# TensorE filler matmuls at the layer borders of a four-layer decoder kernel

## The chip, the cores and the metric

The kernel runs on one NeuronCore of one Trainium2 chip. The metric is the device time of one execution in microseconds, as the median of several runs. A core has a tensor engine (TensorE, PE in the profile; its weight loads are PEld), a vector engine (VectorE, DVE), a scalar engine (ScalarE, ACT), GpSimd (POOL) and a sync engine (SyncE, SP) that issues DMAs. Each engine runs its own list of instructions in order, and engines wait for each other on semaphores.

## The reference, cut to what matters

The input x is 8 sequences of 128 tokens with 128 features in f32. Twelve layers each add to x a function of its layer norm:

```python
x = x + _L0_attn_ref(_layernorm(x, axis=-1), ...)            # L0a: gated, ternary weights
x = x + _L0_xattn_ref(_layernorm(x, axis=-1), ctx, ctx, ...)  # L0x: attention over ctx, rotary
x = x + _L0_ffn_ref(_layernorm(x, axis=-1), ...)              # L0f: 8 experts, top 2
x = x + _L1_attn_ref(_layernorm(x, axis=-1), ...)             # L1a: causal attention
x = x + _L1_xattn_ref(_layernorm(x, axis=-1), ctx, ...)       # L1x: attention with a distance bias
x = x + _L1_ffn_ref(_layernorm(x, axis=-1), ...)              # L1f: 6 experts, top 2, GELU
x = x + _L2_attn_ref(_layernorm(x, axis=-1), ...)             # L2a: linear attention and an inner MLP
x = x + _L2_xattn_ref(_layernorm(x, axis=-1), ctx, ctx, mask, ...)  # L2x: masked attention
x = x + _L2_ffn_ref(_layernorm(x, axis=-1), ...)              # L2f: 16 experts, top 8, SwiGLU
x = x + _L3_attn_ref(_layernorm(x, axis=-1), ...)             # L3a: causal attention, rotary
x = x + _L3_xattn_ref(ctx, ctx, _layernorm(x, axis=-1), ...)  # L3x: one-head attention
x = x + _L3_ffn_ref(_layernorm(x, axis=-1), ...)              # L3f: light and heavy MLP, 50-step router
return x
```

## The kernel before

Everything stays in SBUF. The 8 sequences are split into two groups of 4 (g is 0 or 1), and each group has its own tiles (x, xn, xnT, QT, KT, big and so on) and its own four of the eight PSUM banks (banks_of(g), 512 f32 columns each; bank(i) is the group's i-th). For every engine a generator program(g) lists one group's instructions, layer after layer, and yields a key (layer number, phase) before each piece. weave() merges the two generators in the order of these keys, so each engine's order is written by hand. A step that others wait for is marked with s.step(name), and s.at(name, group) gives the semaphore and the count for pe.wait_ge. Functions ahead() and BEHIND put the entry of group 0 into L0f, L1x, L1f, L2x, L2f and L3x ahead of the end of group 1's previous layer.

Each layer border has the same chain: VectorE adds the layer's output to x (L1289, L1335 or L1347), takes means and variances (L1165 to L1170, mark "var"), GpSimd raises the variance to -0.5 (L332, mark "var_r"), VectorE writes xn (L1360, mark "xn"), TensorE transposes it in four pieces (turn_rows, L415), ScalarE copies it to xnT (L866), and TensorE projects it (mm, L399). The attention layers (attend) loop over 8 half-units per group and end with back() (L468), the normalisation on VectorE (L1245 to L1255, marks "co2" and "co3"), and out_proj (the transposes of co, ScalarE's copy coT, and the projection "y").

The borders that have more in them are L0x (rotary with square roots, marks "qv", "qraw", "qrot", "krot"), L2a (marks "co3", "coT"), L2f (gate_up(c) waits for VectorE's product of the chunk before, "mul"), L3x (a softmax, marks "sub", "exp", "p") and L3f (router: marks "ms", "rs", "xr").

The mask of an attention layer is already applied as the filler is built: a bf16 identity (identb, 128 by 128) times a bf16 constant of 128 by 512 columns, into one bank (masked, L440). An f32 matmul of the source appears in the profile as two MATMUL records, a transpose or a bf16 one as one.

Of the kernel before, what the change touches and what calls it, by code (L numbers as in the profile page):

```python
# [10 lines left out]
ALU = mybir.AluOpType  # L11
# [80 lines left out]
def build(nc, x_d, ctx_d, mask_d, w_d, r_d, c_d, k_d, b_d, out_d, marks):  # L92
# [112 lines left out]
    def four(t):  # L205
        return t.rearrange("p (b d) -> p b d", b=GB)
# [47 lines left out]
    def beat(turn, k=0):  # L254

        return 30 + 10 * turn + k
# [140 lines left out]
    def _(pe):  # L397
# [7 lines left out]
        def program(g):  # L405
# [12 lines left out]
            def project_rows(bk, srcT, weight, name):  # L418
# [2 lines left out]
                    ins = mm(seq(bk, b), srcT[:, b * P:(b + 1) * P], weight)  # L421
                ins.then_inc(*s.step(name))

            def project_cols(bk, srcT, weight, name):

                mm(bank(bk), weight, srcT[:, :]).then_inc(*s.step(name))
# [87 lines left out]

            def out_proj(n, l, weight):
                yield n, (beat(2 * GB - 1, 8) if g == 0 else 130)
                pe.wait_ge(*s.at(f"{l}.co{GB - 1}"))
                turn_rows(3 * g, t.co, "coTp")
                yield n, (beat(2 * GB + 1, 1) if g == 0 else 131)
                pe.wait_ge(*s.at(f"{l}.coT"))  # L520
                project_rows(3 - 3 * g, t.coT, weight, "y")

# [27 lines left out]
            for n, l in enumerate(LAYERS[1:STAGES + 1]):  # L550
# [20 lines left out]
                    ins.then_inc(*s.step("zwp"))  # L571
                if l not in ("L0a", "L3f"):
                    yield n, (BEHIND[l] if g and l in BEHIND else 2)
                    pe.wait_ge(*s.at(f"{l}.xn"))
                    turn_rows(3, xn, "xnTp")
                if l == "L0a":
                    yield n, 2
                    pe.wait_ge(loaded[f"ctx{g}"], 16)
                    turn_rows(3, t.cin, "cTp")
                    yield n, 4  # L580
                    pe.wait_ge(*s.at("L0a.q3"))
                    pe.wait_ge(*s.at("L0a.q3a"))
                    for j in range(3):
                        for b in range(GB):
                            ins = pe.transpose(seq(j, b), t.ta[:, j * GB + b, :], ident)  # L585
                    ins.then_inc(*s.step("q3Tp"))
                    if g == 0:
                        pe.wait_ge(*s.at("L0a.ctxT", 1))
                        pe.wait_ge(*p.at("pre.ones"))
                        pe.wait_ge(*p.at("pre.wabs"))  # L590
                        mm(ps[:, 7 * 512:7 * 512 + 4], ones[:, :], wabs[:, :]).then_inc(*p.step("wsum"))
                    yield n, 6
                    pe.wait_ge(*p.at("pre.wtern"))
                    pe.wait_ge(*s.at("L0a.q3T"))
                    for j in range(3):
                        for b in range(GB):
                            ins = mm(seq(j, b), t.qT3[:, j, b * P:(b + 1) * P], wtern[:, j * P:(j + 1) * P])
                    ins.then_inc(*s.step("ifg"))
                    if g == GROUPS - 1:
                        yield n, 7  # L600
                        pe.wait_ge(*p.at("pre.gwn"))
                        pe.transpose(bank(3)[:, 0:E2], gwn[:, :], ident[0:E2, 0:E2]).then_inc(*p.step("gwTp"))
                    yield n, 12.5
                    pe.wait_ge(*s.at("L0a.ctxT"))
                    if g == 0:
                        pe.wait_ge(loaded["L0x"], 16)
                    pe.wait_ge(*s.at("L0a.ms1"))
                    project_rows(2, ctxT, w("L0x_wk"), "k")
                    yield n, 14
                    if g == GROUPS - 1:  # L610
                        pe.wait_ge(*p.at("pre.gwT"))
                    pe.wait_ge(*s.at("L0a.qo"))
                    pe.wait_ge(*s.at("L0a.qoa"))
                    turn_rows(3, t.ta, "qoTp")
                    yield n, 16
                    pe.wait_ge(*s.at("L0a.qoT"))
                    for b in range(GB):
                        ins = mm(seq(1, b), t.qT3[:, 0, b * P:(b + 1) * P], wtern[:, 3 * P:4 * P])
                    ins.then_inc(*s.step("y"))
                if l in ("L0x", "L3a"):  # L620
                    yield n, 4
                    pe.wait_ge(*s.at(f"{l}.xnT"))
                    project_rows(0, xnT, w(f"{l}_wq"), "q")
                    if l == "L3a":
                        project_rows(1, xnT, w("L3a_wk"), "k")
                        project_rows(2, xnT, w("L3a_wv"), "v")
                    if l == "L0x" and g == 0:
                        yield n, 6
                        turn_keys()
                    yield n, 8  # L630
                    pe.wait_ge(*s.at(f"{l}.qrot"))
                    turn_rows(0, t.tc, "QTp")
                    if l == "L3a":
                        pe.wait_ge(*s.at("L3a.krot"))
                        turn_rows(1, t.td, "KTp")
                    elif g == GROUPS - 1:
                        turn_keys()
                    yield n, 20
                    yield from attend(n, l)
                    yield from out_proj(n, l, w(f"{l}_wo"))  # L640
# [56 lines left out]
                if l == "L2a":  # L697
# [28 lines left out]
                    for h in range(MH):  # L726
# [2 lines left out]
                            ins = mm(bank(h)[:, b * (MD + 1):(b + 1) * (MD + 1)], pr[:, GB * h + b, :], t.vv[:, b, h, :])  # L729
                        ins.then_inc(*s.step(f"O{h}"))  # L730
                    yield n, (22, 24.5)[g]
                    pe.wait_ge(*s.at("L2a.co3"))
                    turn_rows(2, t.co, "coTp")
                    yield n, (22.7, 26)[g]
                    pe.wait_ge(*s.at("L2a.coT"))
                    project_rows(3, t.coT, w("L2a_wo"), "y")
                    yield n, (25, 30)[g]
# [12 lines left out]
                if l == "L2f":  # L750
# [11 lines left out]

                    for c in range(LEAD):
                        yield n, 5 + 4 * c
                        gate_up(c)
                    yield n, 16
                    pe.wait_ge(*s.at("L2f.gws"))
# [23 lines left out]
                if l == "L3x":  # L791
# [7 lines left out]
                        ins = mm(seq(3, b), QT[:, b * P:(b + 1) * P], KT[:, b * P:(b + 1) * P])  # L799
                    ins.then_inc(*s.step("S"))  # L800
                    yield n, 10
                    pe.wait_ge(*s.at("L3x.p"))
                    turn_rows(0, pr, "Tp")
                    yield n, 12
# [6 lines left out]
                    pe.wait_ge(*s.at("L3x.coT"))  # L811
                    project_rows(2, t.coT, w("L3x_wo"), "y")
                if l == "L3f":
                    if g == GROUPS - 1:
                        yield n, 3
                        pe.wait_ge(*s.at("L3f.rs", 0))
                        pe.wait_ge(*s.at("L3f.rs"))
                        pe.transpose(bank(2)[0:B, 0:P], rt_s[:, :], ident).then_inc(*s.step("sT"))
# [288 lines left out]
    def _(dve):  # L1107
# [50 lines left out]
        def program(g):  # L1158
# [169 lines left out]
            def mix(n, l, experts, banks, phase):  # L1328

                for e in experts:  # L1330
# [6 lines left out]
                    if e == experts[len(experts) // 2 - 1]:  # L1337
# [3 lines left out]
                        dve.tensor_tensor(x[:, :, :], four(bank(3)), x[:, :, :], ALU.add).then_inc(*s.step())  # L1341
                        dve.wait_ge(*s.last())
                dve.wait_ge(*s.last())
                if l == "L0f":
                    yield n, 199
                    dve.wait_ge(*s.at(f"L0f.sum{E0 - 2}"))
                    dve.tensor_tensor(x[:, :, :], four(t.hid[:, 0, :]), x[:, :, :], ALU.add).then_inc(*s.step())  # L1347
                    dve.wait_ge(*s.last())

            for n, l in enumerate(LAYERS[1:STAGES + 1]):  # L1350
# [438 lines left out]
```

## Time and profile before

| | |
|---|---|
| time, 3 runs | 690.33 us median (690.32 to 691.32) |
| span of the profiled execution | 688.3 us |
| mean granted TensorE clock | 0.902 |
| PE busy | 548.8 us (80%), 4258 instructions |
| PEld busy | 375.4 us (55%) |
| DVE busy | 468.2 us (68%) |
| ACT busy | 259.3 us (38%) |
| POOL busy | 98.3 us (14%) |
| chain that ended last | PE 64%, DVE 19%, ACT 10%, POOL 2%, issue 2%, DMA 1% |

The span is from the first to the last instruction of one execution. A granted clock of 1.0 is 2.4 GHz and one of 0.5 is 1.2 GHz. In a row of the timeline the first number is the start in us, the second the time of the merged group in us, then come engine, line, operation, output and inputs, shapes and count; in brackets stands how long the engine was idle before and what released it.

### The profile page before, as it was taken

To read this page: it belongs to the slowest core of one execution; us is meant where nothing else is said; L and a number is where in the kernel's file an instruction comes from. 1 tells how busy PE (TensorE), PEld (TensorE's weight loads), DVE (VectorE), ACT (ScalarE), POOL (GpSimd) and SP (SyncE) were. 2 spreads that over 40 slices of the span, in tenths; PEclk is the share of its full clock that TensorE was granted. 3 is DMA by queue.
4 is the path that set the end of the run, shared out by engine and by line. 5 is a ranking of instruction groups with operands and counts; after the bars stand their busy time and mean duration, and the time that the engine had idled before them with its cause. 6 is when DMAs were issued, how large, how long until landed. Compare 5 with 4: busy or idle time off the path is not lost.

```text
span 688.3 us, 10667 instructions
## 1 busy us (share of the span) xinstructions
PE 548.8 (80%) x4258; PEld 375.4 (55%) x4265; DVE 468.2 (68%) x1200; ACT 259.3 (38%) x422; POOL 98.3 (14%) x101
## 2 busy tenths in 40 slices
PE   1436489787689899968996889997799968998487
PEld 0325255686355656655775765556345654565335
DVE  7688688757588777765246745886644378866685
ACT  2365544315244434435332423453321124442270
POOL 5021220004310051000002014200100012002120
PEclk9756699969899999998997999999899989998779
DMA  8900000000000000000000000000000000000001
GB/s 281 371 0 2 0 1 2 1 1 1 0 1 2 1 1 1 2 1 1 0 2 1 0 1 1 1 2 1 0 1 0 1 0 2 1 2 0 0 0 31
DMA packets 6720, 12.40 MB, mean 18 GB/s; under 512 B 528, under 2 KB 4880, under 8 KB 6288
## 3 DMA queue, kind: packets, MB, share of 16 engines
q1 hardware_dynamic: 6672, 11.73, 4.7%
q8 instruction: 33, 0.54, 0.3%
q14 instruction: 15, 0.12, 0.1%
HBM read 11.21 MB, written 0.52 MB: 17 GB/s over the span
## 4 chain that ended last, share of the span: by engine, by line
PE 64%; DVE 19%; ACT 10%; issue 2%; POOL 2%; DMA 1%; SPq 1%; DVEq 0%; ACTq 0%
PE ps L399 47%; PE ps L452 11%; ACT big L897 5%; PE ps L415 4%; DVE st L1165 2%; PE ps L468 2%; DVE big L1276 1%; DVE mx L1272 1%; POOL rs L332 1%; DVE xn L1360 1%; DMA co<-in_ctx 1%; DVE x L1289 1%; PE ps L585 1%; DVE mv L1168 1%; ACT xnT L866 1%
## 5 line engine op out<-in xcount | busy, mean ns | idle before, releaser
L897 ACT ACTIVATE big<-ps 128x1024 f32<-128x1024 f32 x80 | 81.8, 1024 | 109.0 <-PE ps L452 109.0
L1272 DVE TENSOR_REDUCE mx<-ps 128x8 f32<-128x1024 f32 x80 | 97.5, 1219 | 27.9 <-PE ps L399 27.9
L1276 DVE TENSOR_TENSOR big<-ps,mx 128x1024 f32<-128x1024 f32 x80 | 98.0, 1225 | 6.9
L452 PEld LDWEIGHTS ps<-kt,big 128*128 128x128 f32 x640 | 71.0, 141 | 39.0 <-DVE big L1276 28.2
L452 PE MATMUL ps<-kt,big 128*128 128x128 f32 x640 | 85.2, 276 | 5.6 <-DVE big L1276 5.6
L332 POOL TENSOR_TENSOR rs<-ve,negh 128x4 f32<-128x4 f32 x26 | 26.4, 1015 | 393.1 <-DVE ve L1170 393.0
L399 PE MATMUL ps<-xnT,wt 128*128 128x512 f32 (+1 forms) x140 | 73.2, 654 | 5.9 <-DVE big L1552 2.8
L399 PEld LDWEIGHTS ps<-wt,big 128*128 128x128 f32 (+1 forms) x480 | 56.0, 191 | 8.5 <-issue 7.9
L399 PE MATMUL ps<-wt,big 128*128 128x128 f32 (+1 forms) x480 | 60.3, 279 | 0.0
L399 PE MATMUL ps<-big,vaug 128*32 128x128 f32 x1280 | 51.5, 279 | 10.9 <-ACT big L897 10.9
L351 POOL TENSOR_TENSOR KTm<-qk,kt 128x512 f32<-128x512 f32 x34 | 37.4, 1107 | 105.2 <-PE ps L399 62.3
L399 PE MATMUL ps<-bt 128*128 128x512 bf16 (+1 forms) x185 | 48.5, 352 | 1.3 <-issue 0.9
L399 PE MATMUL ps<-KTm,qk 32*128 32x512 f32 x320 | 46.6, 652 | 0.0
L866 ACT ACTIVATE xnT<-ps 128x512 f32<-128x512 f32 (+1 forms) x40 | 19.6, 489 | 71.1 <-PE ps L415 66.2
L399 PEld LDWEIGHTS ps<-big,vaug 128*32 128x32 f32 x1280 | 30.1, 109 | 29.0 <-ACT big L897 22.5
L399 PEld LDWEIGHTS ps<-xnT,wt 128*128 128x128 f32 (+1 forms) x140 | 26.0, 204 | 32.8 <-issue 21.3
L1335 DVE SCALAR_TENSOR_TENSOR x<-ps,gw,x 128x128 f32<-128x128 f32 x80 | 22.3, 344 | 29.8 <-PE ps L399 29.1
L399 PE MATMUL ps<-wt,xnT 128*128 128x128 f32 (+2 forms) x256 | 38.3, 312 | 4.1 <-ACT xnT L866 2.7
L1289 DVE TENSOR_TENSOR x<-ps,x 128x512 f32<-128x512 f32 x16 | 11.1, 692 | 44.4 <-PE ps L399 44.4
L399 PEld LDWEIGHTS ps<-wt,xnT 128*128 128x128 f32 x256 | 36.9, 229 | 7.2 <-ACT xnT L866 4.2
L1360 DVE TENSOR_SCALAR xn<-x,mv,rs 128x128 f32<-128x128 f32 x96 | 28.1, 357 | 9.0 <-POOL rs L332 8.3
L415 PE MATMUL ps<-kt,xn 128*128 128x128 f32 x80 | 17.1, 353 | 19.7 <-DVE xn L1360 19.6
(275 smaller groups left out, 772.1 us busy)
## 6 DMA issues: line engine op xcount, KB each, us to landing
wt<-in_weights SPq DMA_DIRECT2D x1, 1664.0 KB, 17.2
wt<-in_weights SPq DMA_DIRECT2D x1, 1603.0 KB, 12.0
wt<-in_weights SPq DMA_DIRECT2D x6, 256.0 KB, 11.1
bt<-in_bconsts SPq DMA_DIRECT2D x1, 1024.0 KB, 8.5
rowt<-in_rows SPq DMA_DIRECT2D x1, 975.0 KB, 6.7
wt<-in_weights SPq DMA_DIRECT2D x1, 832.0 KB, 13.5
wt<-in_weights SPq DMA_DIRECT2D x1, 608.0 KB, 18.4
wt<-in_weights SPq DMA_DIRECT2D x1, 580.0 KB, 5.6
```

Of the source, the lines that this page charges most:

```text
L332: pool.tensor_tensor(out, src, negh[:, :], ALU.pow).then_inc(*s.step(name + "_r"))
L351: pool.tensor_tensor(t.KTm[:, b % 2, :, :], keys_of(t, b), own_head(), ALU.mult).then_inc(*s.step(f"keys{b}"))
L399: return pe.matmul(out, lhsT, rhs, start=start, stop=stop, **k)
L415: ins = pe.transpose(seq(bk, b), src[:, b, :], ident)
L452: ins = pe.transpose(heads_of(pair(g, u % 2))[:, j // HG, j % HG, :], pr[:, (u % 2) * HH + j, :], ident)
L866: act.activation(out, src, ACT.Copy).then_inc(*s.step(name))
L897: act.activation(PT[:, half * HH:(half + 1) * HH, :].rearrange("p (i j) k -> p i j k", i=2), heads_of(pair(g, half)), ACT.Exp, scale=SCALE ...
L1272: dve.tensor_reduce(top, S, AX.X, ALU.max).then_inc(*s.step())
L1276: dve.tensor_tensor(pr[:, half * HH:(half + 1) * HH, :].rearrange("p (i j) k -> p i j k", i=2), S, top.unsqueeze(3).to_broadcast([P, 2, HG ...
L1289: dve.tensor_tensor(x[:, :, :], four(bank(bk)), x[:, :, :], ALU.add).then_inc(*s.step(name))
L1335: dve.scalar_tensor_tensor(x[:, b, :], bank(banks[e])[:, b * P:(b + 1) * P], gw[:, b, e:e + 1], x[:, b, :], ALU.mult, ALU.add).then_inc(*s ...
L1360: dve.tensor_scalar(xn[:, b, :], x[:, b, :], t.mv[:, b, 0:1], t.rs[:, b:b + 1], ALU.subtract, ALU.mult).then_inc(*s.step("xn"))
```

## The change

A helper filler(k, out) issues k matmuls of identb and identb repeated four times (bf16, 128 by 512 columns) into a bank whose content nobody needs at that point; filler_behind(name, ...) first waits for a named step of another engine, then issues them. No output of a filler is read. There are 176 of them: 13 at the entry of L0x, L1a, L2a and L3a for group 0 (5 behind the previous layer's x, 4 behind var, 4 behind var_r), 10 or 5 at the end of each of the five attention layers for group 1 (8 or 3 before the wait for co3, 2 before the wait for coT), 2 behind the transposes of xn in L0f, L1f, L2f and L3x for each group, 21 in L0x, 8 inside L2a, 7 in L2f, 8 in L3x and 24 in L3f for group 0. Two marks are added on VectorE (L0f.x and L1f.x) so that they can be waited for. Apart from these and the waits of filler_behind no instruction is added, removed or moved.

```diff
--- before.py
+++ after.py
@@ -420,6 +420,15 @@
                 for b in range(GB):
                     ins = mm(seq(bk, b), srcT[:, b * P:(b + 1) * P], weight)
                 ins.then_inc(*s.step(name))
+
+            def filler(k, out):
+
+                for _ in range(k):
+                    mm(out, identb, identb.unsqueeze(1).to_broadcast([P, HG, P]))
+
+            def filler_behind(name, k, out, group=None):
+                pe.wait_ge(*s.at(name, group))
+                filler(k, out)
 
             def project_cols(bk, srcT, weight, name):
 
@@ -514,9 +523,13 @@
 
             def out_proj(n, l, weight):
                 yield n, (beat(2 * GB - 1, 8) if g == 0 else 130)
+                if g == GROUPS - 1:
+                    filler(8 if LAYERS[n + 2] in ("L0f", "L1f", "L2f") else 3, banks_of(0)(0))
                 pe.wait_ge(*s.at(f"{l}.co{GB - 1}"))
                 turn_rows(3 * g, t.co, "coTp")
                 yield n, (beat(2 * GB + 1, 1) if g == 0 else 131)
+                if g == GROUPS - 1:
+                    filler(2, banks_of(0)(0))
                 pe.wait_ge(*s.at(f"{l}.coT"))
                 project_rows(3 - 3 * g, t.coT, weight, "y")
 
@@ -571,8 +584,14 @@
                     ins.then_inc(*s.step("zwp"))
                 if l not in ("L0a", "L3f"):
                     yield n, (BEHIND[l] if g and l in BEHIND else 2)
+                    if g == 0 and l in ("L0x", "L1a", "L2a", "L3a"):
+                        filler_behind(f"{LAYERS[n]}.x", 5, bank(3))
+                        filler_behind(f"{l}.var", 4, bank(3))
+                        filler_behind(f"{l}.var_r", 4, bank(3))
                     pe.wait_ge(*s.at(f"{l}.xn"))
                     turn_rows(3, xn, "xnTp")
+                    if l in ("L0f", "L1f", "L2f", "L3x"):
+                        filler(2, bank(0))
                 if l == "L0a":
                     yield n, 2
                     pe.wait_ge(loaded[f"ctx{g}"], 16)
@@ -628,12 +647,19 @@
                         yield n, 6
                         turn_keys()
                     yield n, 8
+                    if l == "L0x":
+                        if g == 0:
+                            filler_behind("L0x.qv", 5, bank(3))
+                            filler_behind("L0x.qraw", 5, bank(3))
+                        else:
+                            filler(5, bank(3))
                     pe.wait_ge(*s.at(f"{l}.qrot"))
                     turn_rows(0, t.tc, "QTp")
                     if l == "L3a":
                         pe.wait_ge(*s.at("L3a.krot"))
                         turn_rows(1, t.td, "KTp")
                     elif g == GROUPS - 1:
+                        filler(6, bank(3))
                         turn_keys()
                     yield n, 20
                     yield from attend(n, l)
@@ -729,9 +755,12 @@
                             ins = mm(bank(h)[:, b * (MD + 1):(b + 1) * (MD + 1)], pr[:, GB * h + b, :], t.vv[:, b, h, :])
                         ins.then_inc(*s.step(f"O{h}"))
                     yield n, (22, 24.5)[g]
+                    if g:
+                        filler(4, bank(3))
                     pe.wait_ge(*s.at("L2a.co3"))
                     turn_rows(2, t.co, "coTp")
                     yield n, (22.7, 26)[g]
+                    filler(2, bank(3))
                     pe.wait_ge(*s.at("L2a.coT"))
                     project_rows(3, t.coT, w("L2a_wo"), "y")
                     yield n, (25, 30)[g]
@@ -762,6 +791,8 @@
 
                     for c in range(LEAD):
                         yield n, 5 + 4 * c
+                        if c == 2 and g == 0:
+                            filler(7, bank(2))
                         gate_up(c)
                     yield n, 16
                     pe.wait_ge(*s.at("L2f.gws"))
@@ -799,6 +830,9 @@
                         ins = mm(seq(3, b), QT[:, b * P:(b + 1) * P], KT[:, b * P:(b + 1) * P])
                     ins.then_inc(*s.step("S"))
                     yield n, 10
+                    if g == 0:
+                        filler_behind("L3x.sub", 4, bank(0))
+                        filler_behind("L3x.exp", 4, bank(0))
                     pe.wait_ge(*s.at("L3x.p"))
                     turn_rows(0, pr, "Tp")
                     yield n, 12
@@ -811,6 +845,13 @@
                     pe.wait_ge(*s.at("L3x.coT"))
                     project_rows(2, t.coT, w("L3x_wo"), "y")
                 if l == "L3f":
+                    if g == 0:
+                        yield n, 2
+                        filler_behind("L3x.x", 4, bank(3))
+                        filler_behind("L3f.var", 5, bank(3))
+                        filler_behind("L3f.var_r", 5, bank(3))
+                        filler_behind("L3f.xn", 5, bank(3))
+                        filler_behind("L3f.ms", 5, bank(3))
                     if g == GROUPS - 1:
                         yield n, 3
                         pe.wait_ge(*s.at("L3f.rs", 0))
@@ -1341,10 +1382,12 @@
                         dve.tensor_tensor(x[:, :, :], four(bank(3)), x[:, :, :], ALU.add).then_inc(*s.step())
                         dve.wait_ge(*s.last())
                 dve.wait_ge(*s.last())
+                if l == "L1f":
+                    marks[g, "L1f.x"] = marks[g, f"L1f.x{E1 - 1}.{GB - 1}"]
                 if l == "L0f":
                     yield n, 199
                     dve.wait_ge(*s.at(f"L0f.sum{E0 - 2}"))
-                    dve.tensor_tensor(x[:, :, :], four(t.hid[:, 0, :]), x[:, :, :], ALU.add).then_inc(*s.step())
+                    dve.tensor_tensor(x[:, :, :], four(t.hid[:, 0, :]), x[:, :, :], ALU.add).then_inc(*s.step("x"))
                     dve.wait_ge(*s.last())
 
             for n, l in enumerate(LAYERS[1:STAGES + 1]):
```

## Rows read from the trace of the kernel before

**Rows 1.** The page, its second part: 40 equal slices of the span, tenths busy or granted.

```profile
PE   1436489787689899968996889997799968998487
PEclk9756699969899999998997999999899989998779
```

**Rows 2.** Stretches with low granted clock: us, busy (x count) by engine, PEclk, DMA.

```profile
61.97:85.86 23.89, 12.83 (x54) 8.23 (x55) 17.31 (x39) 11.33 (x17) 4.83 (x5) 0.64 0.00 0
137.06:150.72 13.66, 11.93 (x52) 10.88 (x52) 7.46 (x36) 1.19 (x2) 1.01 (x1) 0.50 0.00 1
174.60:181.43 6.83, 3.83 (x11) 2.43 (x12) 3.83 (x23) 1.19 (x2) 2.05 (x2) 0.50 0.00 1
307.73:314.55 6.82, 6.13 (x19) 4.00 (x18) 5.01 (x27) 0.82 (x2) 1.01 (x1) 0.50 0.00 0
365.75:376.00 10.25, 7.08 (x20) 5.67 (x21) 5.43 (x19) 2.48 (x3) 4.20 (x4) 0.50 0.01 2
399.88:403.30 3.42, 2.87 (x13) 2.87 (x14) 0.51 (x3) 1.37 (x2) 0.00 (x0) 0.50 0.00 0
488.63:492.04 3.41, 3.41 (x5) 0.90 (x5) 0.95 (x3) 2.63 (x4) 0.00 (x0) 0.50 0.00 0
498.87:502.29 3.42, 3.42 (x5) 1.35 (x4) 2.36 (x12) 0.60 (x1) 0.00 (x0) 0.50 0.00 0
553.49:560.31 6.82, 4.77 (x21) 4.40 (x22) 3.67 (x17) 1.19 (x2) 1.68 (x2) 0.50 0.00 0
625.16:632.00 6.84, 6.15 (x18) 3.69 (x17) 3.89 (x14) 1.88 (x3) 3.15 (x3) 0.50 0.00 0
638.82:645.64 6.82, 5.11 (x23) 4.72 (x24) 2.66 (x11) 1.79 (x3) 0.00 (x0) 0.50 0.00 0
652.47:662.71 10.24, 6.02 (x13) 2.64 (x14) 8.28 (x53) 6.89 (x15) 4.22 (x4) 0.50 0.00 0
```

**Rows 3.** Timeline, four bf16 matmuls of 512 columns each, at either clock.

```profile
81.31 1.91 PE L399 MATMUL ps<-bt 128*128 128x512 bf16 x4
568.53 1.03 PE L399 MATMUL ps<-bt 128*128 128x512 bf16 x4
```

**Rows 4.** Timeline, PE, group 1 transposes of co in L0x and in L2x.

```profile
137.42 1.11 PE L415 MATMUL ps<-kt,co 128*128 128x128 f32 x4 [2.74 <-DVE co L1255]
479.20 0.66 PE L415 MATMUL ps<-kt,co 128*128 128x128 f32 x4 [2.74 <-DVE co L1255]
```

**Rows 5.** Timeline, PE, entry of L0x: transposes of xn, projection of q.

```profile
63.63 0.66 PE L415 MATMUL ps<-kt,xn 128*128 128x128 f32 x4 [1.86 <-DVE xn L1360]
65.37 3.58 PE L399 MATMUL ps<-wt,xnT 128*128 128x128 f32 x16
```

**Rows 6.** Timeline, L0f: gates and experts of group 0, of group 1; gates read.

```profile
142.83 7.19 PE L399 MATMUL ps<-wt,xnT 128*128 128x8 f32 x32 [0.69 <-ACT xnT L866]
151.55 3.84 PE L399 MATMUL ps<-wt,xnT 128*128 128x8 f32 x32 [0.69 <-ACT xnT L866]
152.71 0.19 DVE L1297 TENSOR_TENSOR lg<-ps,rowt 128x32 f32<-128x32 f32 x1 [3.88 <-PE ps L399]
```

**Rows 7.** Timeline, PE, L1f: first expert of group 0.

```profile
311.44 3.50 PE L399 MATMUL ps<-xnT,wt 128*128 128x512 f32 x4
```

**Rows 8.** Timeline, PE, L2a: feature projections of both groups.

```profile
370.95 9.57 PE L399 MATMUL ps<-zw,xnT 128*128 128x256 f32 x32
```

**Rows 9.** Timeline, PE, L2f: third gate and up chunks, both groups.

```profile
498.42 5.40 PE L399 MATMUL ps<-xnT,wt 128*128 128x512 f32 x8 [2.80 <-DVE big L1552]
```

**Rows 10.** Timeline, PE, L3a: projections of q, k and v, both groups.

```profile
557.54 6.85 PE L399 MATMUL ps<-wt,xnT 128*128 128x128 f32 x48
```

**Rows 11.** Timeline, PE, L3x: weighted values of both groups.

```profile
642.55 3.43 PE L399 MATMUL ps<-big,tc 128*128 128x128 f32 x16
```

**Rows 12.** L3f: piece of the chain (start, us, what); timeline, last router step.

```profile
659.10 11.05 PE ps L399 x20
677.87 0.28 DVE L1650 TENSOR_TENSOR rt_e<-rt_b,rt_r 8x128 f32<-8x128 f32 x1
```

## The prediction

> **What bounds the kernel now.** I read the page's slices first: PE's digits are 8 and 9 in the attention loops and 4 to 7 at the borders between layers, and PEclk drops just there [rows 1]. Then I asked for the granted clock by stretches and cut them where it changes. Behind the first layer there are twelve stretches with a low clock, 102.4 us in all, and in eleven of them it stands at 0.50, which is 1.2 GHz [rows 2]. In every one TensorE had been idle for some us while VectorE, GpSimd and ScalarE did the layer norm, a softmax or a gate. Outside them the clock is 1.0, so attention loops and expert loops have nothing to gain. What a low clock costs is seen best where both groups do the same work: gates and three experts take 7.19 us for group 0 and 3.84 us for group 1 [rows 6], four masks 1.91 against 1.03 us, four transposes 1.11 against 0.66 us [rows 3, 4]. So the question at each border is which part of PE's slow work the next layer waits for, and whether the fillers keep the clock up without being late themselves.
>
> **What the fillers cost.** Four matmuls of the filler's shape take 1.03 us at the high and 1.91 us at the low clock [rows 3]; their starts are some 0.22 and 0.43 us apart, as the last one's way through the array is in these times too. 176 fillers are then 39 us of PE at the high clock, against 688.3 - 548.8 = 139.5 us in which PE is idle. They are placed ahead of waits, and where the wait behind them is longer than they are, they cost nothing. Two behind the transposes of xn take 0.43 us while ScalarE's copy and its hand-over leave PE 0.69 us idle [rows 6]: nothing. The eight ahead of co3 take 1.7 us in an idle time of 2.74 us [rows 4]: nothing. Seven in L2f take 1.5 of 2.80 us [rows 9]: nothing. Cover is too short at two places. At the entry of L0x 13 fillers (2.8 us) stand in an idle time of 1.86 us, and x is ready before PE arrives [rows 5]: +0.95 us. In L2a two fillers stand directly ahead of group 1's y, whose coT is already there: +0.4 us. The added waits are on steps that the old wait for xn, qrot, p or xr includes, so nothing queued behind them on PE is held longer than before. VectorE, ScalarE, GpSimd and the DMA queues get no new instruction or wait; two named marks on VectorE are free. Were the clock low, a filler would be 0.43 us and these covers fail: that is the rival below.
>
> **What a held clock gives, border by border.** The bound of each is half the PE time of its stretch [rows 2]: 73.6/2, less what is already fast in the first one, about 35 us. The path takes less of it:
> - L0x: q's projections 3.58 to 1.8 us [rows 5], less the 0.95; before the first scores the transposed keys (0.45), four masks (0.9) and as much again in scores (0.9) [rows 3, 4]. -3.1.
> - L0x to L0f: the transposes of co (0.45), y (8 records; 16 such take 3.43 us at the low clock [rows 11], so 0.85 less), transposes of xn (0.45), gates and experts 7.19 to 3.84 (3.35), group 1's transposes (0.45) [rows 4, 6]. -5.5. VectorE idled 3.88 us for group 1's gates [rows 6], so it follows.
> - L0f to L1a: transposes and the first projections, of 3.83 us busy [rows 2]; -1.4.
> - L1x to L1f: the first expert's 3.50 us [rows 7] fall by 1.75, gates and transposes by 0.6; -2.35 of at most 3.07.
> - L1f to L2a: VectorE waits for the first quarter of the 9.57 us of feature projections [rows 8], all of which is slow; with the transposes -2.2. Behind that VectorE is busy without a break, so more of PE's 3.5 us isn't worth anything.
> - inside L2a: 1.1 of at most 1.4, less the 0.4 of the two fillers; -0.65.
> - L2f: in 488.63 to 492.04 PE is wholly busy, but the next chunk waits for VectorE's product; I take 0.25 of 1.7. In 498.87 to 502.29 all 8 records of [rows 9] are on the path: -1.7. Together -1.95.
> - L2f to L3a: transposes and q of group 0 (a sixth of the 48 records [rows 10]), then VectorE's rotations bind; -1.45 of 2.4.
> - L3a to L3x: 6.15 us busy, but group 1's xn comes at its own time; -1.5 of 3.1.
> - L3x: transposes and 3.43 us of weighted values [rows 11]; -1.8 of 2.55.
> - L3f: from 659.10 PE has no gap for 11.05 us [rows 12] and is slow to 662.71: -2.6 of 3.0. What is late next is the router, whose last step ends at 678.15 [rows 12]. PE asks for it only in the second half of group 1's y, at the very end of the layer, so I take PE's asking to stay behind it; nearly all of the room is used up.
> Sum: -24.5 us, with bounds of -35 (all slow PE time on the path) and 0.
>
> **Does the clock hold?** The trace has no filler in an idle border. What it shows is that the same idle time can go either way: after 2.74 us group 1's transposes of co run slow in L0x (1.11 us) and fast in L2x (0.66 us) [rows 4]. So fillers that cut such a stretch into pieces should mostly hold it, and some borders will still fall. I take as lost: L0f to L1a, where x comes late and PE is idle before the first filler (no 1.4, and eight fillers at 0.43 us between var and xn, about 1.1 late); half of L3f (1.3), since PE idles again behind its last transposes; and 2.0 for one more border of mean size. That leaves 24.5 - 5.8 = 18.7 us.
>
> The Trainium skill bears on this twice, and no term above needs it. "TensorE: Matmul & The Clock Gate", section Terms, prices a throttled time at that time times one minus its share of the clock; with the lengths and clocks of [rows 2] that would be about 48 us and 642 us, an estimate by that page. The rows speak for half of it, as PE is idle in 29 us of those stretches and VectorE sets part of the rest. The same page, "Part 4: PE-mode transpose", states that transposes don't count as activity for the gate in the way that matmuls do; this speaks for borders that fall in spite of some work in them, and for matmuls as fillers. No row here separates the two.
>
> **Rivals.**
> 1. The clock holds at few borders (the idle pieces between x, var, var_r and xn are still too long, or fillers put off a fall instead of preventing it). The L0x to L0f border, the one with the most fillers in one block, and two or three small ones remain: -5.5, -2.5, against +1 of late fillers: 690.3 - 7 = 683.3. For it: the two fates of one idle time [rows 4]. Against it: the fillers fill half or more of most idle pieces.
> 2. The clock holds everywhere, and PE's earlier work lets the engines behind it start earlier too: -24.5 to -28, about 664. Against it: VectorE's own chain, which sets L2a, L3a and L3x.
> 3. Slower: the fillers don't lift the clock at all, and run at 0.43 us each in front of real work. L0x: 13 take 5.6 us against 1.86 idle, +3.7. L1a, L2a, L3a: the eight behind var and var_r take 3.4 us where some 2.3 us are free, +1.1 each. The pairs behind xn's transposes, 0.86 against 0.69 us [rows 6], eight times +0.17. L2a +0.8. Sum about +9: 699. It decides from the point where lateness (9) exceeds what the borders that do hold give back; a third of the 24.5 us is enough to cancel it. Against it: 4 masks of the same form stand in the attention loops, where the clock is high all along.
> 4. The change doesn't do what it says, for instance because a filler's wait is met too late to matter: then 690, a chance of 3 in 100.
>
> **How the numbers follow.** The profiled execution spans 688.3 us and the median is 690.33, so 2.0 us lie around the span and stay. Forecast: 690.3 - 18.7 = 671.6 us, chance 0.67, by itself 666 to 678 (one or two borders more or fewer). Rival 1: 0.15, rival 2: 0.09, rival 3: 0.06, rival 4: 0.03. The range reaches to both neighbours and leaves out half of each: 663.5 to 683.5. Within 0.2% (1.4 us, about what a measurement of this kernel can tell from no change) is rival 4 alone. Faster 0.91, same 0.03, slower 0.06.
>
> **What would show it.** Twelve low stretches become four or five, and the mean granted clock rises from 0.902 to 0.95 or more. Gates and experts of group 0 in L0f take 3.9 us as those of group 1 do; VectorE's wait before group 1's gates goes. Fillers start 0.22 us apart. PE busy rises by 39 us and falls by what runs faster. At the entry of L0x the transposes of xn follow the fillers without a gap. The prediction is wrong if low stretches still stand at most borders, or if they are gone and the borders are as long as before because VectorE or ScalarE set them.

## The result

The changed kernel takes 670.0 us (median of 4 runs, 667.1 to 671.91) against 690.33 us (4 runs, 688.23 to 691.32): a ratio of 0.972, 95% interval 0.969 to 0.976. The forecast was 671.6 us. The profiled execution was the longest of the four (671.91 us), its span 670.1 against 688.3 us; so the trace explains 18.2 of the 20.3 us. Two executions further on were in a slower state of the chip, one of the kernel without fillers (845.6 us) and one of the kernel before (699.8 us), and the ratios below leave them out (the medians include them, which moves these by less than 0.5 us).

The page of the changed kernel; first the engine's busy time and then the 40 slices, to be held against [rows 1]:

```profile
span 670.1 us, 11020 instructions
PE 561.8 (84%) x4434; PEld 370.8 (55%) x4441; DVE 467.6 (70%) x1200; ACT 260.0 (39%) x422; POOL 98.5 (15%) x101
...
PE   1426689878999999988998889998799978998787
...
PEclk9967999998999999999999999999999999999989
```

PEclk is 9 nearly everywhere; the mean granted clock is 0.971 instead of 0.902. There are 176 more PE instructions, as many as fillers, and PE is busy only 13 us longer, as the fillers' time is mostly made up for by the real work that runs faster. Behind L0a four low stretches are left against the twelve of [rows 2], where the forecast had four or five; the last 2 us of each span are low too and left out. The first row of the next fence is for comparison, the others are these four (columns as in [rows 2]):

```profile
62.00:149.51 87.51, 74.03 (x701) 48.21 (x699) 72.02 (x150) 35.77 (x56) 10.42 (x10) 1.00 0.00 1
149.51:156.34 6.83, 6.28 (x30) 6.10 (x29) 3.94 (x15) 5.17 (x20) 2.50 (x2) 0.50 0.01 2
166.58:169.99 3.41, 3.18 (x8) 1.09 (x9) 3.27 (x21) 0.00 (x0) 1.02 (x1) 0.50 0.01 2
552.28:555.70 3.42, 3.42 (x13) 0.82 (x10) 0.77 (x2) 1.88 (x2) 1.54 (x1) 0.50 0.00 0
641.03:644.44 3.41, 3.37 (x4) 1.13 (x5) 3.08 (x19) 3.00 (x4) 0.00 (x0) 0.50 0.00 0
```

Two of them are new: in the trace of the kernel before the clock was high at the experts of L0f (149.51 here) and at the first masks and scores of L3a (552.28 here).

The L0x to L0f border, timeline of PE and the first read of group 1's gates on VectorE:

```profile
130.66 1.89 PE L399 MATMUL ps<-bt 128*128 128x512 bf16 x8
133.57 0.66 PE L415 MATMUL ps<-kt,co 128*128 128x128 f32 x4 [1.02 <-DVE co L1296]
134.06 0.59 PE L399 MATMUL ps<-bt 128*128 128x512 bf16 x2
134.91 1.16 PE L399 MATMUL ps<-wt,coT 128*128 128x128 f32 x8 [0.26 <-ACT coT L907]
135.91 0.60 PE L415 MATMUL ps<-kt,xn 128*128 128x128 f32 x4
136.34 0.59 PE L399 MATMUL ps<-bt 128*128 128x512 bf16 x2
137.19 3.84 PE L399 MATMUL ps<-wt,xnT 128*128 128x8 f32 x32 [0.26 <-ACT xnT L907]
...
142.15 3.84 PE L399 MATMUL ps<-wt,xnT 128*128 128x8 f32 x32 [0.26 <-ACT xnT L907]
...
143.63 0.19 DVE L1338 TENSOR_TENSOR lg<-ps,rowt 128x32 f32<-128x32 f32 x1
```

The bf16 rows are the fillers. The idle time ahead of the transposes of co is 1.02 us instead of 2.74 [rows 4], that ahead of gates and experts 0.26 instead of 0.69 us, and the real work behind them is not late. Gates and experts of group 0 take 3.84 instead of 7.19 us [rows 6]. VectorE reads group 1's gates 9.1 us earlier than before (143.63 against 152.71), and no longer waits for them.

To place the gain I took instructions that both traces have on VectorE and subtracted their starts. This difference is the lead of the changed kernel. The table has the lead over the kernel before, after each border, and its change (all in us):

| stretch | forecast term | lead after it | change |
|---|---|---|---|
| L0x | -3.1 | 3.86 | -3.86 |
| L0x to L0f | -5.5 | 9.08 | -5.22 |
| experts of L0f | none | 6.33 | +2.75 |
| L0f to L1a | taken as lost, +1.1 | 7.66 | -1.33 |
| L1x to L1f | -2.35 | 9.98 | -2.32 |
| L1f to L2a | -2.2 | 12.19 | -2.21 |
| inside L2a | -0.65 | 13.04 | -0.85 |
| L2f | -1.95 | 15.08 | -2.04 |
| L2f to L3a | -1.45 | 16.36 | -1.28 |
| first scores of L3a | none | 14.71 | +1.65 |
| L3a to L3x | -1.5 | 16.65 | -1.94 |
| L3x | -1.8 | 18.03 | -1.38 |
| L3f | -1.3 of 2.6 | 18.14 | -0.11 |

### The profile page after: what moved, and what is told of

Read it like the earlier page. It is cut to its first block, busy times and chain, and to the rows that moved or that the text cites. A ratio compares the mean times of both kernels' runs of the same rounds, so it can differ in the third digit from the quotient of the medians.

```text
span 670.1 us, 11020 instructions
## 1 busy us (share of the span) xinstructions
PE 561.8 (84%) x4434; PEld 370.8 (55%) x4441; DVE 467.6 (70%) x1200; ACT 260.0 (39%) x422; POOL 98.5 (15%) x101
## 4 chain that ended last, share of the span: by engine, by line
PE 59%; DVE 23%; ACT 11%; POOL 2%; issue 2%; DMA 1%; SPq 1%; DVEq 0%; ACTq 0%
PE ps L399 43%; PE ps L461 11%; ACT big L938 5%; DVE st L1206 3%; PE ps L415 3%; PE ps L477 2%; DVE xn L1403 2%; POOL rs L332 2%; DVE big L1317 1%; DVE mx L1313 1%; DVE x L1330 1%; DMA co<-in_ctx 1%; DVE mv L1209 1%; PE ps L604 1%; DVE ve L1211 1%
## 5 line engine op out<-in xcount | busy, mean ns | idle before, releaser
L399 PE MATMUL ps<-bt 128*128 128x512 bf16 (+1 forms) x361 | 94.0, 369 | 9.1 <-DVE ve L1211 3.1
L399 PE MATMUL ps<-xnT,wt 128*128 128x512 f32 (+1 forms) x140 | 66.5, 602 | 4.8 <-DVE big L1595 2.6
L399 PEld LDWEIGHTS ps<-bt 128*128 128x128 bf16 x368 | 32.3, 99 | 47.1 <-issue 18.5
L399 PEld LDWEIGHTS ps<-big,vaug 128*32 128x32 f32 x1280 | 30.1, 109 | 29.0 <-ACT big L938 22.5
L399 PEld LDWEIGHTS ps<-xnT,wt 128*128 128x128 f32 (+1 forms) x140 | 23.8, 187 | 28.3 <-issue 19.1
L399 PE MATMUL ps<-wt,xnT 128*128 128x128 f32 (+2 forms) x256 | 34.0, 291 | 3.1 <-DVE big L1551 1.5
L399 PEld LDWEIGHTS ps<-wt,xnT 128*128 128x128 f32 x256 | 32.7, 207 | 6.7 <-ACT xnT L907 3.0
```

Source lines behind the costliest of these rows:

```text
L399: return pe.matmul(out, lhsT, rhs, start=start, stop=stop, **k)
```

## The experiments

The theory: everything comes from TensorE's granted clock, and it takes wide matmuls in the idle times to hold it. The rivals: the gain comes from the added waits; any instruction on TensorE will do; the borders aren't separate; fillers cost more than the table shows. Each ratio is to runs of the kernel before on the same chip.

**Waits without fillers.** The fillers are left out, nothing else.

```diff
             def filler(k, out):
-                for _ in range(k):
-                    mm(out, identb, identb.unsqueeze(1).to_broadcast([P, HG, P]))
+                return
```

> The changed kernel with all 176 filler matmuls left out, its added waits kept. Theory (the gain is TensorE's clock alone): as the kernel before, 690 us, within 1 us, and the low-clock stretches of before return at the same borders. Rival A (part of the gain is that TensorE has already passed the earlier semaphores when xn comes, or sits on the waits differently): 3 us or more below 690.

Measured: 690.65 us, ratio 0.999 (0.996 to 1.003). The waits do nothing that can be told from noise, and the gain is the fillers'. Its profiled execution, with a span of 684.1 us, shows more. Stretch and timeline of PE at the L0x to L0f border:

```profile
139.92:153.34 13.42, 9.45 (x78) 8.22 (x76) 11.20 (x59) 2.27 (x7) 1.01 (x1) 1.00 0.00 1
```

```profile
137.12 0.66 PE L415 MATMUL ps<-kt,co 128*128 128x128 f32 x4 [2.74 <-DVE co L1295]
...
140.74 3.84 PE L399 MATMUL ps<-wt,xnT 128*128 128x8 f32 x32 [0.69 <-ACT xnT L906]
```

Without one filler, behind the same 2.74 us of idle time as in [rows 4], the clock stayed up here, where it had fallen in the profiled execution of the kernel before. So which borders fall differs between executions of the same work, and a border's term is what it costs when it falls, not what it costs every time. In the runs that the comparisons use, the kernel before took 685.6 to 694.7 us.

**Narrow fillers.** As many instructions, 8 columns each.

```diff
-                    mm(out, identb, identb.unsqueeze(1).to_broadcast([P, HG, P]))
+                    mm(out[:, 0:8], identb, identb[:, 0:8])
```

> All 176 fillers kept as instructions, each with 8 instead of 512 columns. The theory (clock, and for that the streamed columns of the fillers): 690 us, within 1.5 us, mean granted clock near 0.90. Rival B (any instruction on TensorE keeps the clock up, or an engine that isn't idle starts the real matmuls sooner): most of the 20 us gain remains, 670 to 675 us, clock 0.97.

Measured: 687.71 us, ratio 0.997 (0.994 to 1.001), mean clock 0.909 in the profiled execution. 176 more instructions with weight loads don't hold the clock; the same number with 512 columns does. As a narrow filler is also much shorter, this doesn't tell columns from busy time. The median lies 2.1 us under that of the kernel before (689.81 us here), where I had allowed 1.5; the interval includes no difference.

**Transposes as fillers.** Two f32 transposes of the identity in the place of each matmul.

```diff
-                for _ in range(k):
-                    mm(out, identb, identb.unsqueeze(1).to_broadcast([P, HG, P]))
+                for _ in range(2 * k):
+                    pe.transpose(out[:, 0:P], ident, ident)
```

> Each filler matmul is replaced by two f32 transposes of the identity, 128 columns each (four transposes took 0.66 us, so two are about 0.22 us apart as one filler is). If TensorE's clock takes transposes for work as it takes matmuls: 670 us, within 3 us, clock 0.97. If, as the Trainium skill (TensorE: Matmul & The Clock Gate, Part 4) states, transposes don't count in the same way: 688 us or more, for the fillers then run at 0.43 us a pair in front of real work, up to 699 us.

Measured: 670.98 us, ratio 0.970 (0.966 to 0.975), clock 0.971. The L0x to L0f border:

```profile
130.74 1.91 PE L427 MATMUL ps<-kt 128*128 128x128 f32 x16
133.64 0.66 PE L415 MATMUL ps<-kt,co 128*128 128x128 f32 x4 [1.00 <-DVE co L1296]
...
137.27 3.84 PE L399 MATMUL ps<-wt,xnT 128*128 128x8 f32 x32 [0.25 <-ACT xnT L907]
```

Sixteen transposes (line 427 of this kernel is the filler) take the time of eight fillers, and hold the clock as well: VectorE's leads agree with those of the changed kernel within 0.2 us to the end. Here the measurement decides against the page: the Trainium skill ("TensorE: Matmul & The Clock Gate", Part 4: PE-mode transpose) says that the full clock doesn't engage for transposes, as they don't count as activity in the same way. F32 transposes held it in this kernel, and they raised it too. In this trace the clock is low from 166.71 to 170.12 us, at the entry of L1a, and TensorE does nothing else in this time than these transposes, the first 15 of this row:

```profile
166.91 4.58 PE L427 MATMUL ps<-kt 128*128 128x128 f32 x26 [2.30 <-DVE x L1390]
```

Behind it the clock is 1.0, while the rest of them run.

**Twice as many.** Each group of fillers twice as long (range(2 * k)).

> Every filler group twice as long (352 matmuls). Theory: the clock is held at a few more borders (at most the 4 us still lost), but the fillers no longer fit into the idle times: at the entry of L0x 26 take 5.6 us (+2.8 more), pairs behind xn's transposes become 0.87 against 0.69 us (8 times +0.2), 16 ahead of co3 take 3.5 against 2.7 us (3 times +0.8), the 8 and 8 behind var and var_r fill 3.5 of 2.3 us (3 times +1.2), 14 in L2f 3.0 against 2.8. Sum about +12, so 675 to 684 us. Rival (lateness is hidden behind other engines): 670 or below.

Measured: 677.05 us, ratio 0.981 (0.976 to 0.985), clock 0.996. The clock is held as good as everywhere in the profiled execution, and the kernel is 5.5 to 7 us slower than with half of them. The entry of L0x:

```profile
61.58 6.16 PE L399 MATMUL ps<-bt 128*128 128x512 bf16 x26
67.57 1.04 PE L415 MATMUL ps<-kt,xn 128*128 128x128 f32 x8
```

The transposes of xn start at 67.57 instead of 63.99 us, and VectorE keeps these 3.5 us; 13 more fillers at 0.22 us are 2.8 of them, and the rest is the clock's, which rose at 62.3 instead of 60.8 us here. At the other borders doubling costs 0.1 to 1 us each, in L3f about 2, and where the clock is now held, or is low for a shorter time, 1.1 to 1.6 us come back (experts of L0f, L3a, L3f). 677 lies in the expected 675 to 684, at its low end: the sum of 12 us was too large.

**Half as many.** 95 matmuls, range((k + 1) // 2).

> Every filler group halved (8 to 4, 5 to 3, 4 to 2, 2 to 1 and so on, 95 matmuls in all). Theory (the clock needs enough work in each idle time): several borders fall again and half to two thirds of the gain is left, 676 to 682 us. Rival (any break in the idle time is enough): 670 us or, with less lateness, 669.

Measured: 680.78 us, ratio 0.986 (0.982 to 0.990), clock 0.924 in the profiled execution: half of the gain, as expected (676 to 682). The L1x to L1f border:

```profile
299.76 1.57 PE L399 MATMUL ps<-wt,coT 128*128 128x128 f32 x8 [0.47 <-ACT coT L907]
...
304.60 3.76 PE L399 MATMUL ps<-xnT,wt 128*128 128x512 f32 x4
```

One filler ahead of coT and four ahead of co3 don't hold it: y is slow in part, the first expert wholly (3.76 us, as the 3.50 of [rows 7]). With 95, 176 and 352 fillers the times are 681, 670 to 671.5 and 677: too few lose the clock, too many are late.

**One border alone.** Only the 14 fillers of the L0x to L0f border. Against the changed kernel:

```diff
-                if g == GROUPS - 1:
+                if g == GROUPS - 1 and l == "L0x":
                     filler(8 if LAYERS[n + 2] in ("L0f", "L1f", "L2f") else 3, banks_of(0)(0))
...
-                    if l in ("L0f", "L1f", "L2f", "L3x"):
+                    if l in ("L0f",):
                         filler(2, bank(0))
```

(and the other groups left out)

> Only the 14 fillers of the L0x to L0f border kept (8 ahead of co3 and 2 ahead of coT for group 1, 2 behind the transposes of xn for each group). Theory by my sum: 5.2 to 5.5 us faster than the kernel before in a trace where this border is slow before, so 684.5. Theory of luck (a border that is held only moves the fall to another one): 1 to 3 us faster. No gain at all would say that the borders aren't separate terms.

Measured: 685.39 us against 690.4 us, ratio 0.995 (0.991 to 0.998): 5 us by the medians, as the term says; but the interval reaches from 1 to 6 and so takes in the 1 to 3 us of the theory of luck. In the trace VectorE gains 5.3 us on the kernel before at this border, gives back 0.9 in the experts of L0f, where the clock falls from 152.88 to 156.29 us, and ends 4.7 us ahead. So the border is worth about its term, and a part of it is lost again right behind it. One such trace doesn't show that the fillers did it: the kernel without any gained 5.2 us at this border in its profiled execution and gave back 1.2. No other border was tested alone; that their terms add up is read from the table and not shown by an experiment.

**L3f.** This border gave 0.11 us of the 1.3. In the changed kernel (PE, then VectorE's wait for the transposed router weights):

```profile
639.64 0.66 PE L415 MATMUL ps<-kt,tc 128*128 128x128 f32 x4 [0.51 <-ACT tc L1125]
641.07 10.94 PE L399 MATMUL ps<-qk,wt 128*64 128x512 f32 x20 [0.78 <-ACT qk L1133]
...
664.19 0.17 DVE L1696 COPY rt_f<-ps 128x8 f32<-128x8 f32 x1 [4.08 <-PE ps L885]
```

The transposes behind the fillers are fast, then PE idles again and the clock falls at 641.03, just ahead of the long block, which takes 10.94 us as it took 11.05 before [rows 12]. The block starts 18.03 us earlier than before, which is the lead on entering L3f, so the fast transposes ahead of it brought nothing by themselves. Either the clock is missing here, or the router binds. Three kernels on one chip:

> The changed kernel once more, beside the next three on the same chip, for comparison: 670 us.

> The 24 fillers of L3f left out, with their waits. In the changed kernel's trace L3f is as long as before (VectorE's lead of 18.03 us on entering it is 18.14 us at the end). Theory X (they hold the clock only up to the router's transposes and lose it before the long block of projections): the same as the changed kernel, 670 us, within 1 us. Theory Y (they hold it in most executions and the profiled one was unlucky): 1.5 to 2.5 us slower.

> Nine more fillers in L3f: 4 behind ms, and 2 and 3 behind the transposes of the normalised rows of each group, where TensorE was idle 1.02, 0.51 and 0.78 us. If the clock is what L3f lacks: the block of 8 slow projections falls from 3.4 to 1.7 us and the kernel by 1.5 to 2.6 us, to 668. If the 50-step router binds as soon as the projections are earlier: less than 0.5 us.

```diff
-                        filler_behind("L3f.ms", 5, bank(3))
+                        filler_behind("L3f.ms", 9, bank(3))
...
                     turn_rows(3, t.tc, "xrTp")
+                    filler(2 + g, bank(0))
```

Measured: the changed kernel 671.51 us (ratio 0.973), without L3f's fillers 670.51 us (0.972), with nine more 669.04 us (0.970). The intervals, each some 0.004 to either side, overlap; so the medians alone don't tell the three apart, and the traces have to. With nine more:

```profile
638.85 0.81 PE L399 MATMUL ps<-bt 128*128 128x512 bf16 x3
639.79 9.31 PE L399 MATMUL ps<-qk,wt 128*64 128x512 f32 x20
```

```profile
661.28 0.17 DVE L1697 COPY rt_f<-ps 128x8 f32<-128x8 f32 x1 [2.44 <-PE ps L886]
```

The block falls to 9.31 us, and the kernel's end follows by the same 1.64 us (its lead over the changed kernel goes from 1.26 us in the router's steps to 2.91 us at the last product). VectorE still waits 2.44 us for PE, so the router doesn't bind. The 24 fillers of L3f as they stand are worth nothing that shows: they fill the time up to ms and leave the last two gaps open.

**More fillers where the clock still falls.**

```diff
+                if l == "L0f":
+                    filler_behind("L0f.lgs", (7, 2)[g], bank(3))
                 pe.wait_ge(*s.at(f"{l}.gw"))
...
+                    if g == 0 and l == "L1a":
+                        filler_behind("L0f.x5.3", 7, bank(3))
...
+                    if l == "L3a" and g:
+                        filler(5, bank(3))
                     pe.wait_ge(*s.at(f"{l}.qrot"))
                     turn_rows(0, t.tc, "QTp")
                     if l == "L3a":
+                        if g:
+                            filler(6, bank(3))
```

(and the nine of L3f; 36 in all, where the expectation counts 38)

> The changed kernel with 38 more fillers where its traces still show a low clock: 7 and 2 ahead of the transposed gates in L0f (group 0, group 1), 7 ahead of L1a behind VectorE's step x5.3, 5 and 6 in L3a's rotation for group 1, and the 9 of L3f. Theory: L0f gives back the 2.8 us it lost in the profiled execution, L3a up to 1.65, L3f 1.5 to 2.5; together 4 to 6 us less than the changed kernel, 665 us. Rival (a late filler costs what the clock gives): 669 to 671.

Measured: 667.58 us, ratio 0.968 (0.964 to 0.971), on another chip than the run above. That is 3.9 us less than the 671.51 and 2.4 less than the 670.0 of the changed kernel, under the 4 to 6 that were expected. In its trace VectorE gains 2.75 us on the changed kernel in L0f, 1.64 us at the first scores of L3a and 1.64 us in L3f, and gives back 1.42 us in L3x, where the clock now falls.

```diff
                     yield n, 4
+                    if g:
+                        filler(9, bank(0))
+                        filler_behind("pre.wtern", 16, bank(0))
+                        filler_behind("L0a.q3_s", 6, bank(0))
                     pe.wait_ge(*s.at("L0a.q3"))
...
+                    if g == 0:
+                        filler(8, bank(0))
+                        filler_behind("L0a.qo_s", 4, bank(0))
+                    else:
+                        filler(5, bank(0))
                     pe.wait_ge(*s.at("L0a.qo"))
```

> The same with 48 more fillers in L0a, where the clock is low from 24 to 61 us in every trace: 31 ahead of group 1's first transposes, 17 ahead of both groups' transposes for the output projection. TensorE's slow work there is q3 transposes of group 1 (2.8 us), k and v projections (3.9 and 3.3 us) and smaller ones, of which VectorE waits only for a part. Theory: 1.5 to 4 us less than the kernel with 38 more, 662. Rival (VectorE alone sets L0a): the same as that kernel, within 1 us.

Measured: 665.15 us, ratio 0.965 (0.961 to 0.968), beside the 667.58: 2.4 us less, within the expected 1.5 to 4, though 662 was not reached. (The expectation has the clock low from 24 to 61 us in every trace; in four of them, the changed kernel's among them, it was high in parts of this time.) In the traces it is 1.5 us ahead behind the first transposes and 2.2 us ahead once it is through L0x. The kernel with 36 more and this one differ at L3x, where their code is the same. First the one with 36 more, then this one; the gap ahead of group 0's transposes of the probabilities is 1.13 us in both, ahead of group 1's 1.06:

```profile
619.48 0.66 PE L415 MATMUL ps<-kt,big 128*128 128x128 f32 x4 [1.13 <-DVE big L1664]
621.20 1.11 PE L415 MATMUL ps<-kt,big 128*128 128x128 f32 x4 [1.06 <-DVE big L1664]
622.11 3.08 PE L399 MATMUL ps<-big,tc 128*128 128x128 f32 x16
```

```profile
617.26 0.66 PE L415 MATMUL ps<-kt,big 128*128 128x128 f32 x4 [1.13 <-DVE big L1673]
618.98 0.65 PE L415 MATMUL ps<-kt,big 128*128 128x128 f32 x4 [1.06 <-DVE big L1673]
619.48 2.07 PE L399 MATMUL ps<-big,tc 128*128 128x128 f32 x16
```

Same distances, one slow and one fast: what decides is not in this stage's work alone.

**Seven more in L3x** (behind exp 7 instead of 4, and 4 for group 1; the kernel that they are added to has 260 fillers, not the 262 of the expectation):

> The kernel of 262 fillers with 7 more in L3x, 3 behind the exponentials for group 0 and 4 ahead of group 1's wait for p, where TensorE was idle 1.13 and 1.06 us in two traces. Of these two, one lost the clock there at 621.05 us (the weighted values took 3.08 us) and the other, with the same order of work at the same distances, did not (2.07 us). Theory: the loss there, 1.4 us in some of the executions, goes: 664.5 us, and the spread of the runs narrows. Rival (the idle time was long enough already, the loss comes from elsewhere): 665 to 666 us.

Measured: 664.68 us, ratio 0.966 (0.962 to 0.970), six runs from 664.06 to 666.47 us. Against the 665.15 us (663.89 to 666.48), measured with other runs of the kernel before, this is no difference that can be told, and the spread is as it was, so the expected narrowing didn't come. The gaps shrank in its trace to 0.49 and 0.20 us, and the weighted values took 2.07 us, as they already did in the trace with 260. Both are some 5 us ahead of the change and 25 us ahead of the kernel before; the clock of the kernel with L0a's fillers in 40 slices:

```profile
PEclk9959999999999999999999999999999999999999
```

## Why the prediction was right

**The mechanism** is shown: without fillers or with narrow ones the time is that of before, with streamed work of either kind it is 670 to 671.5, and the granted clock moves with it. In one point the prediction read its rows too simply: PE had not been idle for some us ahead of every low stretch. Ahead of 399.88 it was 1.47 us, and ahead of 488.63 pauses of 0.69, 0.41 and 0.69 us in the 7 us before.

**The terms by border.** All borders together gave 22.5 us in the trace against the 24.5 of the sum. The nine whose clock held gave 21.1 us against 20.5, and six of their terms were within 0.3 us. L0x was 0.8 us better. Its term counted 0.95 us of lateness from 13 fillers in an idle time of 1.86 us; in the trace of the changed kernel it is 0.36:

```profile
58.04 3.31 PE L399 MATMUL ps<-wt,ctxT 128*128 128x128 f32 x16
61.19 2.97 PE L399 MATMUL ps<-bt 128*128 128x512 bf16 x13
63.99 0.60 PE L415 MATMUL ps<-kt,xn 128*128 128x128 f32 x4
65.36 2.01 PE L399 MATMUL ps<-wt,xnT 128*128 128x128 f32 x16
```

The transposes of xn start at 63.99 instead of 63.63 us [rows 5]. The clock happened to rise earlier, at 60.76 us, so that PE was through with v's projections 0.6 us sooner. That fillers are late where the cover is short was right in kind, and the doubled kernel shows it (3.5 us).

**L3f** was sized too large. I took 2.6 us for a held clock there, and half of it as lost, since PE idles again behind its last transposes. Held, it gives 1.64 us more; unheld 0.11. The last transposes were indeed the place where the clock fell. The room ahead of the router was larger than I took it to be: 2.44 us of it are left.

**What is lost.** I took 5.8 us off: L0f to L1a, half of L3f, and one more border of mean size. In place of these the trace shows 2.5 us missing in L3f and 4.4 us lost at places that were fast before and had no term, in L0f and L3a, while L0f to L1a gave 1.33 us although the clock was low from 166.58 to 169.99 (8 of its 13 fillers, those that start up to 170 us):

```profile
166.81 3.44 PE L399 MATMUL ps<-bt 128*128 128x512 bf16 x8 [2.30 <-DVE x L1390]
```

There the slow fillers were through in time, and the clock rose before the real work. So the allowance was near in sum (5.8 us, where the trace lies 6.4 under the 24.5) and wrong in place; that the total came out so near is in part luck. I looked only where the clock was low before. At the new fall in L0f PE had idled 1.85 us for the gates; in the kernel before (the second fence) it was 1.54 us:

```profile
147.84 0.60 PE L552 MATMUL ps<-kt,gw 128*8 128x128 f32 x4 [1.85 <-DVE gw L1366]
149.06 0.62 PE L552 MATMUL ps<-kt,gw 128*8 128x128 f32 x4 [0.62 <-DVE gw L1366]
150.24 6.73 PE L399 MATMUL ps<-wt,xnT 128*128 128x128 f32 x32 [0.55 <-ACT big L1061]
```

```profile
156.93 0.60 PE L539 MATMUL ps<-kt,gw 128*8 128x128 f32 x4 [1.54 <-DVE gw L1325]
159.33 3.98 PE L399 MATMUL ps<-wt,xnT 128*128 128x128 f32 x32 [0.57 <-ACT big L1020]
```

The 32 records take 6.73 us instead of 3.98. This goes with the border that was held just before, and is no chance of one trace. There VectorE has become the later one: it reads group 1's gates 1.48 us behind the start of PE's block (143.63 against 142.15), where it was 1.16 us before (152.71 against 151.55), so PE waits 0.3 us longer for what it makes of them. In all nine traces in which the L0x to L0f border kept its clock and no fillers stand ahead of these gates, that of the kernel without fillers included, PE idles 1.85 to 1.87 us here and the clock falls in the experts; in the two in which the border fell (the kernel before and the one with half the fillers) it is 1.54 us and the clock stays. VectorE gives back 0.9 to 2.8 us by it in these nine. The kernels with fillers there don't have this stretch. The fall in L3a stands only in one trace of the changed kernel and in that of the transposes, and not in the other trace of the changed kernel: that one is chance.

**The rule for a throttled time** (the Trainium skill, "TensorE: Matmul & The Clock Gate", section Terms), by which all low stretches were worth 48 us, overstates: 20.3 us were measured, and 23 with all but one of the stretches behind L0a gone (the kernel with 36 more). It takes every slow moment for lost, but PE was idle in 29 of the 102 us, and part of its work ran ahead of what VectorE could take [rows 2].

**Rivals.** The clock held at most borders, so rivals 1, 3 and 4 are out; rival 3's lateness appears only with twice the fillers. Rival 2 isn't what the changed kernel does, as four low stretches remain. Its 664 is nearly reached (665.15) only with more fillers in L0f, L3a and L3f, and in L0a, which the sum of terms leaves out; without those of L0a it is 667.6.

**Open**: why one and the same idle time lets the clock fall in one execution and not in the next. No run here varied that alone. Open too is whether every border's term would stand alone, as only one was tested.

## What to carry to other kernels

Where the granted clock falls at a stage's border and real matmuls on the path run slow behind it, filling TensorE's idle time with wide matmuls or transposes of constants can pay: price it as half of the slow work that another engine waits for, not as half of the slow time. Put the fillers behind the other engines' steps, so that each piece ends before the input of the real work is there, and fill the last gap ahead of it; half the number lost half the gain here, and twice the number cost 5.5 to 7 us. A border that is held changes which engine is late behind it: look for the next idle time there, as the one of L0f, which grew from 1.54 to 1.85 us and took back 2.75 us. Judge it by several executions, as a border that was lucky in one trace can fall in the next.

## What the runs showed of the hardware

F32 transposes hold the clock as wide matmuls do (670.98 against 670.0 us), and in one stretch it rose on them alone (170.12 us), while as many matmuls of 8 columns don't (687.71 us). The clock went either way behind equal idle times and equal work of the stage: 2.74 us at the L0x border in two executions, 1.13 and 1.06 us in L3x in two others. Eight fillers at the high clock take 1.89 us, and two of them in the 0.69 us between ScalarE's copy and the next matmul don't delay it.
